# A Mamba block beside a mixture of experts: two products, then two scans on VectorE, and B's spreads as jobs in the ring of three banks

## The chip, the cores and the metric

The kernel runs on one core of one Trainium2 chip. The metric is device time of one execution, in microseconds (us). Three executions of the kernel before took 312.34, 308.81 and 311.08 us: median 311.08.

## The reference, cut to what matters

The input is 8 sequences of 256 tokens with 128 features, so 2048 tokens. All is float32.

```
xn = layernorm(x)
# s: Mamba block on xn
xr = rmsnorm(xn) * norm_w;   xi, z = split(xr @ W_in)          # 256 channels each
xc = silu(causal_conv4(xi) + conv_b)
dt, B, C = split(xc @ W_x, [64, 80]);   dt = softplus(dt @ W_dt + b_dt)
h[t] = exp(dt * A) * h[t-1] + (dt * xc * B)[t]                  # 256 channels x 16 states
y = (sum over states of h * C + D_skip * xc) * silu(z);   s = xn + y @ W_out
# g: eight experts, the best two of each token, on xn
p = softmax(xn @ Wg);  scores = top-2 of p, normalised to sum 1
g = silu(sum over e of scores[e] * (relu(xn @ W1[e] + b1[e]) @ W2[e] + b2[e]))
out = x + s * g
```

## The kernel before, in words

The tokens go in 4 chunks of 512 tokens (two sequences). Channels times states of a chunk are 4096 recurrences. They are laid on 128 partitions as 4 states by 32 channels, two blocks of 32 channels to an instruction, so one **unit** is 128 partitions by 1024 elements and a chunk has 16 units, 64 in all. A pair of blocks (pair 0 to 3) meets four quads of states. Two units in a row, on two pairs, share a quad and so a spread of B.

A unit n passes through five steps on four engines:

- ScalarE makes the decays: two `decay` instructions of 128x512, `exp(negA * dt)` (L561), into `dec`, a ring of three.
- TensorE spreads four rows of B over the partitions: `spread_B` (L998), one matmul of 512 columns for two units, into one of the two PSUM banks `pB`.
- VectorE multiplies `dt*xc` by that B (`times_B`, the **product**, L879) into the two banks `pdbu`, and runs the **scan** (L892) over `dec` and `pdbu` into `hs`, a ring of three.
- GpSimd multiplies by C (`times_C`, L390) into `hc`, a ring of four.
- TensorE sums over the states in the bank `py` (`reduce`, L1017), for two units at once.

`dt` and `dt*xc` reach the partitions as `rep`, repeated by DMAs of 32 partitions (`replicas`, L321), eight for each pair.

Every engine has its own queue and works it in order; semaphores are the only links. The order is written out in slots. A chunk has 32 slots; before the change VectorE runs the product of unit n in slot 2n and its scan in slot 2n+1. Everything else is a **job** or a **step** that TABLE or STEPS puts in a slot: `tr` and `tn` transposes, `xc0`, `xc1` convolution, `z0`, `z1`, `dt`, `v0`, `v1` projections, `gl`, `gs`, `gb` gate and expert bias, `m0a` to `m7b` first and `y0` to `y7` second layers of experts, `o` output. TensorE fills each job (`fill`) into one of three PSUM banks `px`, by turns in the order of the list JOBS, and ScalarE (or VectorE: `by_dve`) empties it (`empty`). A job can be filled only when the job three places ahead of it in JOBS has been emptied:

```
dst = px[j % AUX]
if j >= AUX:
    wait_emptied(pe, *JOBS[j - AUX])
```

The product waits for the scan ahead of it, since both use the same `pdbu`, and the scan waits for its product:

```
dve.wait_ge(scan_done, n)          # in times_B(n)
dve.wait_ge(dbu_done, n + 1)       # in scan(n)
if n >= HS_RING:
    dve.wait_ge(hc_done, n - HS_RING + 1)
```

The router's part on VectorE is `gate`, a generator of five steps for a chunk, whose small instructions wait for one another one by one (`link`). `silu` (slot 10 or 11 of a chunk) has ScalarE load a table, run the SiLUs of the next chunk's `xc` and `z`, and load the table of exp and log again. Ahead of the slots stands a start-up part, PRE_JOBS, which makes the first unit of decays and products from `d0`, `d1`, `x0`, `x1` without `rep`; `keep_busy` has TensorE run matmuls whose result is not used.

## Time and profile before

| | |
|---|---|
| median of three executions | 311.08 us (308.81 to 312.34) |
| the profiled execution | 309.04 us |
| its span, first to last instruction | 307.2 us |
| busy: TensorE, VectorE | 276.6 us, 275.8 us |
| busy: GpSimd, ScalarE | 236.9 us, 224.3 us |
| 64 scans, 63 products on VectorE | 146.2 us, 77.3 us |
| 63 products by C on GpSimd | 149.2 us |
| first scan starts, last scan ends | 30.48 us, 296.83 us |

The busy time of an engine counts each moment once, so instructions that overlap do not count twice. TensorE's matmuls are pipelined and their ends are modelled: its real load is read from the starts of rows that follow one another. In the rows below, square brackets at the end of a row are the idle time of its engine ahead of it and what ended it.

### The profile page before, as it was taken

What the parts mean: (1) busy time and instruction counts of PE and PEld (TensorE: products, weight loads), DVE (VectorE), ACT (ScalarE), POOL (GpSimd) and SP (SyncE); (2) the same over time, 40 slices, a digit from 0 to 9 for tenths busy, and PEclk for the clock granted to TensorE, in tenths of its full rate; (3) what the DMA queues carried; (4) which work ended last, traced back from release to release, by engine and by line L of the source; (5) the groups of instructions that cost most, each with busy time, mean ns of one, the idle gap of its engine ahead of it and who ended that gap; (6) DMA issues with size and microseconds to landing.
All of it is one profiled execution on the core that took longest, in us unless ns stands there. A gap on an engine that the chain in (4) does not pass through costs nothing. (4 is left out here: it accounts for less than half of the span.)

```text
span 307.2 us, 4290 instructions
## 1 busy us (share of the span) xinstructions
PE 276.6 (90%) x1273; PEld 144.9 (47%) x1273; DVE 275.8 (90%) x317; ACT 224.3 (73%) x440; POOL 236.9 (77%) x184
## 2 busy tenths in 40 slices
PE   7996689989999999698999999799998799997992
PEld 5633234534726453136645554235762555561662
DVE  4778899949999999999999899999999999999993
ACT  1495496799994948999688686999666684696640
POOL 6327966359899975667999887668999688869893
PEclk9999979999999999999999999799999999999999
DMA  6938980006065830041470660050938600000002
GB/s 185 292 97 182 231 191 10 0 6 137 0 154 132 194 73 0 0 122 21 104 172 1 139 138 1 4 137 11 206 67 185 150 0 2 0 0 1 3 0 68
DMA packets 16630, 26.23 MB, mean 85 GB/s; under 512 B 4264, under 2 KB 9759, under 8 KB 16608
## 3 DMA queue, kind: packets, MB, share of 16 engines
q1 hardware_dynamic: 15794, 24.78, 34.5%
q0 software_dynamic: 384, 1.05, 1.5%
q8 instruction: 10, 0.16, 0.2%
q10 hardware_dynamic: 430, 0.14, 0.2%
q14 instruction: 12, 0.10, 0.1%
HBM read 8.00 MB, written 1.18 MB: 30 GB/s over the span
## 5 line engine op out<-in xcount | busy, mean ns | idle before, releaser
L390 POOL TENSOR_TENSOR hc<-hs,Ct 128x1024 f32<-128x1024 f32 x63 | 149.2, 2377 | 24.3 <-DVE hs L892 23.9
L892 DVE TENSOR_TENSOR_SCAN hs<-dec,pdbu 128x1024 f32<-128x1024 f32 x64 | 146.2, 2285 | 9.2 <-ACT dec L561 5.1
L561 ACT ACTIVATE dec<-rep,negA 128x512 f32<-128x512 f32 x126 | 86.9, 725 | 7.0 <-DMA rep<-dt_u 4.7
L879 DVE TENSOR_TENSOR pdbu<-rep,pB 128x1024 f32<-128x1024 f32 x63 | 77.3, 1228 | 5.5
L1119 PE MATMUL px<-xnT,w 128*128 128x512 f32 x128 | 64.6, 606 | 6.8 <-ACT xnT L624 2.8
L1125 PEld LDWEIGHTS px<-w,hT 128*128 128x128 f32 x512 | 60.8, 192 | 18.5 <-issue 9.4
L1125 PE MATMUL px<-w,hT 128*128 128x128 f32 x512 | 62.7, 277 | 3.0 <-ACT hT L690 3.0
L690 ACT ACTIVATE hT<-px,cols 128x512 f32<-128x512 f32 x64 | 43.5, 689 | 21.3 <-PE px L1125 10.7
L506 POOL TENSOR_TENSOR acc<-acc,ysc 128x512 f32<-128x512 f32 x29 | 37.6, 1297 | 17.6 <-ACT ysc L679 17.3
L679 ACT ACTIVATE ysc<-px,score 128x128 f32<-128x128 f32 x116 | 32.9, 371 | 14.6 <-PE px L1125 14.5
L1017 PE MATMUL py<-hc,rsel 128*32 128x512 f32 x256 | 39.2, 609 | 2.3 <-POOL hc L390 2.2
L1119 PEld LDWEIGHTS px<-xnT,w 128*128 128x128 f32 x128 | 21.9, 192 | 34.5 <-issue 16.5
L998 PE MATMUL pB<-dtp,sel 128*128 128x512 f32 x64 | 34.3, 618 | 0.5 <-DVE pdbu L879 0.5
L1069 PE MATMUL px<-xrT,wtap 128*128 128x512 f32 x56 | 25.4, 595 | 0.0
L998 PEld LDWEIGHTS pB<-dtp,sel 128*128 128x128 f32 x64 | 10.6, 189 | 19.3 <-issue 16.2
L1017 PEld LDWEIGHTS py<-hc,rsel 128*32 128x32 f32 x256 | 6.1, 109 | 27.4 <-issue 16.1
L1069 PEld LDWEIGHTS px<-xrT,wtap 128*128 128x128 f32 x56 | 10.2, 188 | 11.9 <-issue 10.6
L1076 PE MATMUL px<-xc,wx 128*96 128x512 f32 x16 | 9.3, 714 | 5.6 <-ACT xc L577 4.2
L647 ACT ACTIVATE xv<-px,cols 128x512 f32<-128x512 f32 x6 | 4.1, 686 | 10.6 <-PE px L1069 10.6
L397 POOL TENSOR_TENSOR zr<-zr,xv 128x512 f32<-128x512 f32 x6 | 7.6, 1275 | 4.6 <-DVE xv L853 4.6
L514 POOL TENSOR_TENSOR hs<-hs,hc 128x512 f32<-128x512 f32 x2 | 2.5, 1280 | 10.4 <-ACT hc L717 10.4
L1006 PE MATMUL py<-xc,skip 128*128 128x512 f32 x16 | 9.1, 655 | 1.4 <-DVE sz L901 1.4
(155 smaller groups left out, 275.5 us busy)
## 6 DMA issues: line engine op xcount, KB each, us to landing
rep<-dt_u SPq DMA_DIRECT2D x120, 128.0 KB, 2.4
Ct<-c_rows SPq DMA_DIRECT2D x16, 256.0 KB, 5.0
w<-in_L_ffn_W SPq DMA_DIRECT2D x1, 1024.0 KB
rep<-dt_u POOLq DMA_DIRECT2D x8, 128.0 KB, 4.6
...
```

The lines of the kernel that those rows point to most:

```text
L390: eng.tensor_tensor(hc[:, n % HC_RING], hs[:, n % HS_RING], Ct[:, k % 2, j:j + 1, :].to_broadcast([P, 2, CH]), ALU.mult).then_inc(hc_last ...
L506: pool.tensor_tensor(acc[:, k % 2, :], acc[:, k % 2, :], ysc[:, pool_experts.index((k, e)) % YSC_RING, :], ALU.add).then_inc(acc_added, 1)
L561: act.activation(dec[:, n % DEC_RING, i, :], rep[:, q, 0, :], ACT.Exp, scale=negA[:, q, j:j + 1])\
L679: ins = act.activation(ysc[:, m % YSC_RING, t], src[:, t], ACT.Copy, scale=score[:, k % 2, i, e:e + 1])
L690: ins = act.activation(hT[:, e % 2, b, :], src[:, :], ACT.Relu, bias=cols[:, V_B1 + HB * e + b:V_B1 + HB * e + b + 1])
L879: dve.tensor_tensor(pdbu[:, :, :], rep[:, 2 * pair:2 * pair + 2, 1, :], pB[:, m % 2:m % 2 + 1, :].to_broadcast([P, 2, CH]), ALU.mult).then ...
L892: dve.tensor_tensor_scan(hs[:, n % HS_RING].rearrange("p b t -> p (b t)"), dec[:, n % DEC_RING].rearrange("p b t -> p (b t)"), pdbu[:, :, ...
L998: pe.matmul(pB[:, m % 2, :], sel[:, j].rearrange("p s d -> p (s d)"), dtp[:, k % 2, :], start=True, stop=True)\
L1017: last = pe.matmul(py[r:r + GD, 0, :], rsel[:, :], hc[:, n % HC_RING, i, :], start=False, stop=j == QUADS - 1)
L1069: last = pe.matmul(dst[:, :], wtap[:, t, b * P:(b + 1) * P], xrT[:, :, t:t + SEQ], start=t == 0, stop=t == TAPS - 1)
L1119: last = pe.matmul(dst[:, :], w1[:, e, b * P:(b + 1) * P], xnT[:, k % 2, :], start=True, stop=True)
L1125: last = pe.matmul(dst[:, i * D:(i + 1) * D], hT[:, e % 2, b, i * P:(i + 1) * P], w2[:, e, b, :], start=b == 0, stop=b == HB - 1)
```

## The change

- **VectorE's order.** `at_slot` puts the products of units 2m and 2m+1 in slots 4m and 4m+1 and their scans in slots 4m+2 and 4m+3. `pdbu` has four banks, two for even and two for odd units; a product waits for the scan two units back.
- **B.** `spread_B` and the banks `pB` are gone. The spread for units 2m and 2m+1 is a job `B` in the ring `px`, ahead of the other jobs of slot 4m-2. Nothing empties it but the second product that reads it: its bank comes free when product 2m+1 is done.
- **Start.** `rep` of pair 0 of the first chunk is made by four matmuls (`u0`, `u1`, `e0`, `e1`) and four copies on ScalarE instead of eight DMAs, of which SP issued four and GpSimd four. The first scan stands ahead of the second half's `correction` on VectorE. Eleven of the sixteen matmuls of `keep_busy` go.
- **Tables.** Jobs and steps get new slots. `gate` is 15 steps of one instruction each. The memset of the far value is a step of its own (`far`). `reduce` of units 2i and 2i+1 moves from slot 4i+6 to 4i+7. The last load of the SiLU table moves from slot 124 to 129.

```
-PRE_JOBS = ["tr", "xc0", "xc1", "dt", "x0", "v0", "x1", "v1", "d0", "d1", "tn", "m0a"]
+PRE_JOBS = ["tr", "xc0", "xc1", "dt", "x0", "v0", "B", "x1", "v1", "d0", "d1", "tn", "u0", "u1", "e0", "e1", "m0a"]
...
-    3: ["tr"], 6: ["z1"], 7: ["xc0", "z0"], 9: ["xc1"], 12: ["y0", "y1", "dt"], 13: ["m3a", "tn", "v0"],
...
+    3: ["tr"], 7: ["xc1"], 9: ["xc0", "z0", "z1"], 12: ["dt"], 13: ["y0", "tn", "v0"], 15: ["y1", "gl"], 16: ["m2a"],
...
 START = {
-    "second": [0], "gate": [2, 3, 4, 4, 7], "gate_e": [0], "gate_p": [1, 3, 5],
+    "second": [1], "gate": [1, 1, 3, 3, 5, 5, 5, 5, 6, 7, 7, 8, 8, 8, 10], "gate_e": [0], "gate_p": [1, 7, 7],
 }
+AHEAD = 2
 LEAD = 2
-LAG = 5
+LAG = 7
...
-BUSY = {"row": 8, "rows": 4, "tr": 2, "xc1": 2}
+BUSY = {"row": 3, "xc1": 2}
...
+for m in range(1, UNITS // HALF_PAIRS):
+    SLOTS.setdefault(4 * m - AHEAD, []).insert(0, ("B", m))
...
+def at_slot(n):
+
+    m, r = divmod(n, 2 * HALF_PAIRS)
+    scans = (1, 3) if m == 0 else (2, 3)
+    return r in scans, HALF_PAIRS * m + (r // 2 if m == 0 else r % 2)
...
-        pB = banks("pB", 2)
-        pdbu = banks("pdbu", 2)
+        pdbu = banks("pdbu", 4)
...
         def wait_emptied(eng, job, k):
 
-            if by_dve(job, k):
+            if job == "B" and k > 0:
+                eng.wait_ge(dbu_done, HALF_PAIRS * (k + 1))
+            elif by_dve(job, k):
...
-                dve.wait_ge(B_spread, m + 1)
-                if j == first_quad(k, pair):
+                if j == 0:
                     wait_replicas(dve, k, pair)
-                dve.wait_ge(scan_done, n)
-                dve.tensor_tensor(pdbu[:, :, :], rep[:, 2 * pair:2 * pair + 2, 1, :], pB[:, m % 2:m % 2 + 1, :].to_broadcast([P, 2, CH]),
-                                  ALU.mult).then_inc(dbu_done, 1)
+                if n > 1:
+                    dve.wait_ge(scan_done, n - 1)
+                if m == 0:
+                    wait_emptied(dve, "B", 0)
+                    B = B_first
+                else:
+                    wait_filled(dve, "B", m)
+                    B = bank_of("B", m)
+                at = 2 * (n % 2)
+                dve.tensor_tensor(pdbu[:, at:at + 2, :], rep[:, 2 * pair:2 * pair + 2, 1, :],
+                                  B[:, None, :].to_broadcast([P, 2, CH]), ALU.mult).then_inc(dbu_done, 1)
...
                 if n < 2 * UNITS:
-                    scan(n // 2) if n % 2 else times_B(n // 2)
+                    scanned, unit = at_slot(n)
+                    scan(unit) if scanned else times_B(unit)
...
+                elif job in ("u0", "u1"):
+                    pe.wait_ge(u_done, 1)
+                    last = pe.matmul(dst[:, :], copies(int(job[1])), dt_u[:, 0, 1, :], start=True, stop=True)
+                elif job in ("e0", "e1"):
+                    pe.wait_ge(far_done, 1)
+                    last = pe.matmul(dst[:, :], copies(int(job[1])), dt_u[:, 0, 0, :], start=True, stop=True)
...
-                if n % 4 == 3 and n // 4 + 2 < UNITS // HALF_PAIRS:
-                    spread_B(n // 4 + 2)
-                if n % 4 == 2 and 0 <= (n - LAG) // 4 < UNITS // 2:
+                if (n - LAG) % 4 == 0 and 0 <= (n - LAG) // 4 < UNITS // 2:
                     reduce((n - LAG) // 4)
```

**VectorE, from the end of the first chunk into the second,** around the steps `gate_y` (L901, L931 now) and `o` (L917, L947 now). L879 and L908 now are products, L892 and L922 now are scans; `px1` is a bank of the ring. Before:

```order
L901 TENSOR_TENSOR sz<-py,sz 128x512
L892 SCALAR_TENSOR_TENSOR hs<-dec,pdbu 128x1024
L879 TENSOR_TENSOR pdbu<-rep,pB 128x1024
L892 SCALAR_TENSOR_TENSOR hs<-dec,pdbu 128x1024
L917 TENSOR_TENSOR xn<-px1,xn 128x512
L879 TENSOR_TENSOR pdbu<-rep,pB 128x1024
L892 SCALAR_TENSOR_TENSOR hs<-dec,pdbu 128x1024
L879 TENSOR_TENSOR pdbu<-rep,pB 128x1024
L892 SCALAR_TENSOR_TENSOR hs<-dec,pdbu 128x1024
```

Now:

```order
L931 TENSOR_TENSOR sz<-py,sz 128x512
L884 MEMSET dt_u 128x2
L922 SCALAR_TENSOR_TENSOR hs<-dec,pdbu 128x1024
L947 TENSOR_TENSOR xn<-px2,xn 128x512
L908 TENSOR_TENSOR pdbu<-rep,px1 128x1024 x2
L922 SCALAR_TENSOR_TENSOR hs<-dec,pdbu 128x1024 x2
L908 TENSOR_TENSOR pdbu<-rep,px2 128x1024 x2
L922 SCALAR_TENSOR_TENSOR hs<-dec,pdbu 128x1024 x2
```

Products and scans now come two and two, and each two products read one bank of the ring.

**TensorE, slots 5 to 13 of the first chunk,** where the next chunk's convolution is done. L998 before and L1118 now spread B; L1069 and L1093 are a convolution, L1076 and L1100 the job `dt`, L1017 and L1041 `reduce`, L1125 and L1161 a `y`. Before:

```order
L998 MATMUL pB<-dtp,sel 128x512
L1069 MATMUL px2<-xrT,wtap 128x512 x4
L1055 MATMUL px0<-xrT,win 128x512
L1107 MATMUL px1<-ident,score 32x128
L1069 MATMUL px2<-xrT,wtap 128x512 x4
L1017 MATMUL py<-hc,rsel 32x512 x4
L998 MATMUL pB<-dtp,sel 128x512
L1113 MATMUL px0<-b2d,sT 128x512
L1125 MATMUL px1<-w2,hT 128x128 x8
L1125 MATMUL px2<-w2,hT 128x128 x8
L1076 MATMUL px0<-xc,wx 96x512 x2
```

Now:

```order
L1118 MATMUL px1<-dtp,sel 128x512
L1030 MATMUL py<-xc,skip 128x512
L1041 MATMUL py<-hc,rsel 32x512 x4
L1093 MATMUL px2<-xrT,wtap 128x512 x4
L1093 MATMUL px0<-xrT,wtap 128x512 x4
L1079 MATMUL px1<-xrT,win 128x512
L1079 MATMUL px2<-xrT,win 128x512
L1118 MATMUL px0<-dtp,sel 128x512
L1143 MATMUL px1<-ident,score 32x128
L1041 MATMUL py<-hc,rsel 32x512 x4
L1149 MATMUL px2<-b2d,sT 128x512
L1100 MATMUL px0<-xc,wx 96x512 x2
```

The two convolutions and `z0`, `z1` now all stand between two spreads of B, and `dt` stands in the bank of the next B, so it waits for that B's products.

**ScalarE, right behind the SiLUs of the second chunk.** L561 before and L570 now are decays, L679 and L692 the scaling of an expert's output. Before:

```order
L581 ACT_TABLE_LOAD
L683 ACTIVATE acc<-px0 128x512
L561 ACTIVATE dec<-rep,negA 128x512
L679 ACTIVATE ysc<-px1,score 128x128 x4
L679 ACTIVATE ysc<-px2,score 128x128 x4
L652 ACTIVATE dtp<-px0 96x512
L561 ACTIVATE dec<-rep,negA 128x512
```

Now:

```order
L590 ACT_TABLE_LOAD
L696 ACTIVATE acc<-px2 128x512
L570 ACTIVATE dec<-rep,negA 128x512
L661 ACTIVATE dtp<-px0 96x512
L570 ACTIVATE dec<-rep,negA 128x512
L692 ACTIVATE ysc<-px1,score 128x128 x4
```

The two experts' scalings no longer stand between the two decays of unit 8.

## Rows read from the trace of the kernel before

**Rows 1.** The cores: span, and mean granted TensorE clock.

```profile
core 0: 307.2 us, clock 0.988
```

**Rows 2.** The page: busy us (share of the span) and instructions of each engine.

```profile
PE 276.6 (90%) x1273; PEld 144.9 (47%) x1273; DVE 275.8 (90%) x317; ACT 224.3 (73%) x440; POOL 236.9 (77%) x184
```

**Rows 3.** Windows: us, busy of PE, PEld, DVE, ACT, POOL (instructions), clock, DMA share, GB/s.

```profile
36.63:296.83 260.20, 241.62 (x1138) 124.88 (x1139) 242.77 (x231) 206.16 (x409) 210.85 (x129) 0.99 0.31 71
296.83:307.20 10.37, 4.84 (x39) 3.50 (x37) 5.37 (x12) 0.63 (x1) 4.89 (x3) 0.97 0.18 51
```

**Rows 4.** VectorE by line: busy, mean ns of one, idle ahead of them and its releaser.

```profile
L892 DVE TENSOR_TENSOR_SCAN hs<-dec,pdbu 128x1024 f32<-128x1024 f32 x64 | 146.2, 2285 | 9.2 <-ACT dec L561 5.1
L879 DVE TENSOR_TENSOR pdbu<-rep,pB 128x1024 f32<-128x1024 f32 x63 | 77.3, 1228 | 5.5
```

**Rows 5.** VectorE in order of time: start us, us, line, operation, tiles.

```profile
139.18 2.27 DVE L892 TENSOR_TENSOR_SCAN hs<-dec,pdbu 128x1024 f32<-128x1024 f32 x1
141.37 0.16 DVE L824 TENSOR_REDUCE gmx<-px 128x4 f32<-128x32 f32 x1
...
147.32 0.18 DVE L829 TENSOR_REDUCE gsm<-gex 128x4 f32<-128x32 f32 x1
147.54 0.18 DVE L830 RECIPROCAL gri<-gsm 128x4 f32<-128x4 f32 x1
...
155.78 1.23 DVE L879 TENSOR_TENSOR pdbu<-rep,pB 128x1024 f32<-128x1024 f32 x1
156.92 0.56 DVE L845 TENSOR_TENSOR goh<-iota,gif 128x64 f32<-128x64 f32 x1
...
161.22 2.29 DVE L892 TENSOR_TENSOR_SCAN hs<-dec,pdbu 128x1024 f32<-128x1024 f32 x1
163.61 1.23 DVE L879 TENSOR_TENSOR pdbu<-rep,pB 128x1024 f32<-128x1024 f32 x1
164.93 2.29 DVE L892 TENSOR_TENSOR_SCAN hs<-dec,pdbu 128x1024 f32<-128x1024 f32 x1
```

**Rows 6.** In order of time, all engines, 63 to 68 us.

```profile
63.85 2.17 ACT L679 ACTIVATE ysc<-px,score 128x128 f32<-128x128 f32 x8
...
66.33 0.75 ACT L561 ACTIVATE dec<-rep,negA 128x512 f32<-128x512 f32 x1
...
67.11 2.29 DVE L892 TENSOR_TENSOR_SCAN hs<-dec,pdbu 128x1024 f32<-128x1024 f32 x1 [4.51 <-ACT dec L561]
```

**Rows 7.** TensorE in order of time, 169 to 179 us.

```profile
169.41 1.95 PE L1125 MATMUL px<-w,hT 128*128 128x128 f32 x16
171.19 0.60 PE L1049 MATMUL px<-ident,rl 128*128 128x128 f32 x4
...
172.77 1.07 PE L1017 MATMUL py<-hc,rsel 128*32 128x512 f32 x8
173.77 3.70 PE L1069 MATMUL px<-xrT,wtap 128*128 128x512 f32 x8
177.31 1.02 PE L998 MATMUL pB<-dtp,sel 128*128 128x512 f32 x2
178.16 1.02 PE L1055 MATMUL px<-xrT,win 128*128 128x512 f32 x2
```

**Rows 8.** Window of 20 us, columns as in rows 3.

```profile
160.00:180.00 20.00, 20.00 (x104) 11.75 (x103) 18.36 (x13) 14.61 (x35) 18.60 (x13) 1.00 0.43 96
```

**Rows 9.** GpSimd by line.

```profile
L390 POOL TENSOR_TENSOR hc<-hs,Ct 128x1024 f32<-128x1024 f32 x63 | 149.2, 2377 | 24.3 <-DVE hs L892 23.9
```

**Rows 10.** Windows of 2 us around a pause of TensorE.

```profile
192.00:194.00 2.00, 0.20 (x2) 0.22 (x2) 1.81 (x3) 1.99 (x3) 1.88 (x1) 1.00 0.00 0
194.00:196.00 2.00, 2.00 (x3) 0.59 (x3) 1.90 (x2) 1.98 (x3) 0.65 (x2) 0.50 0.00 0
```

**Rows 11.** ScalarE in order of time: the first decays from rep.

```profile
32.67 1.33 ACT L561 ACTIVATE dec<-rep,negA 128x512 f32<-128x512 f32 x2 [2.23 <-DMA rep<-dt_u]
...
36.43 0.72 ACT L561 ACTIVATE dec<-rep,negA 128x512 f32<-128x512 f32 x1 [2.42 <-DMA rep<-dt_u]
```

More of the change, by code:

```diff
@@ L93 @@
+OWN = {"o"} | {f"{a}{i}" for a in "xdue" for i in range(2)} | {f"y{e}" for e in range(EXPERTS)} | {f"m{e}{b}" for e in range(EXPERTS) for b in "ab"}
 SLOTS = {n: [(j, 0) for j in EARLY[n]] for n in EARLY}
@@ L238, in mamba_moe @@
         c_out, c_in = sem("c_out"), [sem(f"c_in{i}") for i in range(2)]
-        rep_in, rep_soft = [sem(f"rep_in{i}") for i in range(PAIRS)], [sem(f"rep_soft{i}") for i in range(HALF_PAIRS)]
+        rep_in, rep_soft = [sem(f"rep_in{i}") for i in range(PAIRS)], sem("rep_soft")
         e_done, l_done = sem("e_done"), sem("l_done")
@@ L258, in mamba_moe @@
         ov_dram = out.rearrange("b (h p) d -> p (b h) d", p=P)
-        order_a = [job for job in JOBS if not by_dve(*job)]
+        order_a = [job for job in JOBS if not by_dve(*job) and (job[0] != "B" or job[1] == 0)]
         order_v = [job for job in JOBS if by_dve(*job)]
@@ L300, in wait_added @@
                 eng.wait_ge(acc_added, pool_experts.index((k, e)) + 1)
-        def first_quad(k, pair):
-            return 1 if (k, pair) == (0, 0) else 0
         def wait_replicas(eng, k, pair):
-            early = pair < HALF_PAIRS
-            eng.wait_ge(rep_in[pair], N_REP * (k + 1) - (N_REP // 2 if early else 0))
-            if k == 0 and early:
-                eng.wait_ge(rep_soft[pair], N_REP // 2)
+            if (k, pair) == (0, 0):
+                wait_emptied(eng, "e1", 0)
+            elif (k, pair) == (0, 1):
+                eng.wait_ge(rep_in[1], N_REP // 2)
+                eng.wait_ge(rep_soft, N_REP // 2)
+            else:
+                eng.wait_ge(rep_in[pair], N_REP * (k + (pair > 1)) + (N_REP // 2 if pair == 1 else 0))
         def decays(n):
@@ L374, in _ @@
                 for pair in range(PAIRS):
-                    repeat_dt_u(k, pair ^ 1 if k == 0 and pair < HALF_PAIRS else pair)
+                    if (k, pair) != (0, 0):
+                        repeat_dt_u(k, pair)
             for k in range(CHUNKS):
@@ L515, in _ @@
             pool.wait_ge(far_done, 1)
-            for q in (3, 1):
-                replicas(pool, q, True)
+            replicas(pool, 3, True)
             rest_roots()
@@ L555, in decay @@
                 k, j, pair = place(n)
-                if j == first_quad(k, pair) and i == 0:
+                if j == (1 if n < HALF_PAIRS * QUADS and pair == 0 else 0) and i == 0:
                     wait_replicas(act, k, pair)
@@ L612, in empty @@
             def empty(job, k):
-                if job[-1] == "<" or by_dve(job, k):
+                if job[-1] == "<" or job == "B" or by_dve(job, k):
                     return
@@ L740, in _ @@
                     empty(job, k)
+                for _ in steps_at(n, "last_table"):
+                    assert n >= 2 * (UNITS - LEAD) - 1
+                    act.preload_act_table_set("silu_and_others")
+                    silu_of_experts(CHUNKS - 2)
                 for k, b in steps_at(n, "log1p"):
@@ L828, in gate @@
                 dve.wait_ge(gate_exp, k + 1)
-                link(dve.tensor_reduce(gsm[:, :], gex[:, :, :], AX.X, ALU.add))
-                link(dve.reciprocal(gri[:, :], gsm[:, :]))
+                dve.tensor_reduce(gsm[:, :], gex[:, :, :], AX.X, ALU.add).then_inc(gate_step, 1)
+                yield
+                dve.wait_ge(gate_step, done + 2)
+                dve.reciprocal(gri[:, :], gsm[:, :]).then_inc(gate_step, 1)
                 yield
@@ L960, in _ @@
                     correction(k, b)
+                for k, b in steps_at(n, "far"):
+                    set_far(k, b)
                 for k, b in steps_at(n, "times_dt"):
@@ L986, in _ @@
             last.then_inc(cw_spread, 1)
[L987 removed]
             pe.wait_ge(w_rows, 16 * N_ROWS)
[L989 to L999 removed]
+            pe.transpose(pdbu[:, 2, 0:V_END], rows[:, :], ident[0:V_END, 0:V_END]).then_inc(vec_t, 1)
             def skip_xc(k, b):
@@ L1089, in fill @@
                                          start=True, stop=True)
+                elif job == "B":
+                    if k == 0:
+                        pe.wait_ge(selected, N_SELECTED)
+                    wait_emptied(pe, "dt", k // (DB * QUADS))
+                    last = pe.matmul(dst[:, :], sel[:, k % QUADS].rearrange("p s d -> p (s d)"),
+                                     dtp[:, k // (DB * QUADS) % 2, :], start=True, stop=True)
                 elif job in ("x0", "x1"):
```

112 lines of the change are left out of this document (53 added, 59 removed), and 26 rows, old and new, of the table TABLE.

## The prediction

> **What bounds the kernel now.** I read first the span and the totals, then the windows, then VectorE's lines, then its instructions in order of time. The span is 307.2 us [rows 1] and the profiled execution 309.04 us, so 1.84 us lie around it. TensorE and VectorE are both busy 90% [rows 2], which does not say which one sets the time. The windows say more: from the end of the second scan (36.63 us) to the end of the last (296.83 us) VectorE is busy 242.8 of 260.2 us, and behind it come 10.4 us of tail [rows 3]. VectorE's 17.4 idle us are what to look at. Its two big lines hold 9.2 + 5.5 us of them; only 5.1 us are put down to another engine, ScalarE's decays [rows 4]. The other 9.6 us have no releaser: VectorE waits for itself.
>
> The order of time shows how. A scan starts at 161.22 and takes 2.29 us; the product behind it, which needs its banks, starts at 163.61, 0.10 us after the scan's end; the next scan, which needs that product, starts at 164.93, 0.09 us after the product's end [rows 5]. A unit so takes 2.39 + 1.32 = 3.71 us. Where the instruction behind needs nothing of the one ahead, it starts before that one ends: the router's reduction at 141.37, 2.19 us after its scan's start; the comparison at 156.92, 1.14 us after its product's start [rows 5]. So a link from scan to product costs 0.20 us more than no link, one from product to scan 0.18 us more, and a unit without both takes 3.33 us. VectorE sets the time, and about a tenth of a unit is the wait for its own result.
>
> **The change, part by part.**
>
> *Two products, then two scans.* Every product and scan is then followed by an instruction that does not need it. Number of links that go: 5.5 us of idle ahead of products by 0.10 to 0.13 us is some 48; 4.1 us ahead of scans (9.2 less the 5.1) by 0.09 is some 45 [rows 4, 5]. At 0.20 and 0.18 us: 9.6 + 8.1 = 17.7 us. All lies on the path, since VectorE is it. The lower bound is that only the 9.6 us of idle go; nothing is excluded above 17.7. I take 17.7, by the two independent pairs.
>
> Here a rule speaks against the change. The Trainium skill (VectorE: DVE Perf Modes, The DRAIN you can't avoid) says that the next operation does not issue until the pipe is empty and that leaving out semaphores between operations won nothing. By that rule the links would be worth nothing. The page itself adds (Two Vector instructions with no wait between them) that an instruction that is not held starts earlier, and this case's trace agrees with that: 0.08 and 0.09 us before the end of the one ahead, against 0.09 and 0.10 us after it. The measurement decides.
>
> *The router in 15 steps, the far memset apart.* In a chunk some five small instructions wait for one another, like the reciprocal 0.04 us after the end of its reduction (147.50 to 147.54) [rows 5]. With a scan or product between them that is 0.12 us less each: 4 chunks by about 4 links, 2 us. Between 0 and 3; 2 taken.
>
> *The stall at 62 us.* VectorE's longest wait is 4.51 us for the second decay of unit 8, at 66.33 us: ScalarE had come out of its SiLUs and then did eight scalings, 2.17 us, and `dt` ahead of that decay [rows 6]. In the new order the scalings stand behind it, and the scan of unit 8 comes one slot later. This wait should go. What is late next is B: between the spreads for units 4, 5 and for units 8, 9, TensorE has two convolutions of 3.54 us, two `reduce` of 1.0 us, `y0` of 1.78 us, and nine matmuls of 512 columns and 0.85 us (`z0`, `z1`, `gb`, two for `dt`, `v0`, one of skip, two of B), with 0.6 us for transposes: 7.1 + 2.0 + 1.8 + 7.7 + 0.6 = 19.2 us [rows 7]. VectorE needs for four units 13.3 us, with the router 14.0. B runs ahead by 3 to 4 us at most, since its ring stands still until the products ahead are done. So B is late by 1.6 us or more; with the wait of `dt` for the SiLUs and for the bank of a B I take 2.5. Net 4.5 - 2.5 = 2 us won; bounds 0 and 4.5.
>
> *B in the ring.* Before, a spread had two banks of its own. Now it holds one of three from its fill until the second product is done, and TensorE can fill two more jobs behind it and then stands. Everything from the third job to the next B then has to fit under two scans and their company, 4.4 us and more. In most groups it does: three matmuls of 0.85 and a `y` of 1.78 with `reduce`. Where it doesn't, I count as above: behind spread 16 stand from the third job on `m7b`, `y6`, `tr`, `y7` and the next B, 0.85 + 1.78 + 0.6 + 1.78 + 0.85 = 5.9 us, under 5.0 us of scans and one output: 0.9 late; around 18 stand two convolutions again, 1.3 late. Over all 31 spreads, those of the stall above left out, this gives some 3.5 us. TensorE has little in reserve: 20.00 of 20 us busy at 160 to 180 us [rows 8]. Lower bound 0; upper bound by the `y` of 1.78 us that is the common piece, half of one late at every second spread, 14 us.
>
> *GpSimd and ScalarE.* The multiplication by C takes 2.38 us [rows 9], and a scan of an odd unit may start only when that of the unit two back is done. In steady state that one starts with the two products and has 1.14 + 1.14 + 2.19 = 4.5 us for 2.38, a slack of 2.1 us; before it was 3.71 + 1.32 - 2.38, about 2.7. Where an expert's addition and a sum for dt stand together it is used up. I take 1.2 us for such places, bounds 0 and 6. `reduce` a slot later costs nothing: it is hidden under the scans, and at the end its last part waits for the last C product, as before.
>
> *The start.* ScalarE waited 2.42 us for the replicas of pair 0 behind 2.23 us for those of pair 1 [rows 11]. The second wait goes, and eight DMAs with it, four issued by SP and four by GpSimd; for it ScalarE has four copies, of about a decay's 0.72 us, while it would wait for pair 1 anyway. SP's sixteen issues for pairs 2 and 3, queued behind, begin sooner or at the same time. The first wait stays, and with it the second product. As VectorE did the router's part in that time, I take 1 us, between 0 and 2.4. The eleven matmuls less of `keep_busy` I cost at nothing while the clock stays up; what it costs if it does not is a rival below. The tail of 10.4 us [rows 3] stays: the last four instructions of units 62, 63 end in the same chain.
>
> Sum, on the profiled execution: 309.0 - 17.7 - 2 - 2 + 3.5 + 1.2 - 1 = **291.0 us**. The median of before stands 2.0 us above the profiled execution and its runs 3.5 us apart, so for the median of after I say 292.
>
> **The rivals.**
>
> *B late at every spread: slower.* One B for each two units, 31 of them. The links, the router, the stall and the start are worth 20 to 23 us, so at 0.7 us late at each the gain is gone. One thing makes that possible: TensorE standing for a full ring. After 1.8 of 2 us without work (192 to 194 us) its granted clock was 0.50, that is 1.2 of its 2.4 GHz, in the next 2 us [rows 10], and a B and a convolution then take twice as long, while the ring is what made it stand. At 1.0 us each the time is 309 - 22.7 + 31 = 317 us. For it: TensorE's full window [rows 8], a ring now shared by 45 jobs a chunk instead of 37. Against it: counted by group, TensorE's work is less than VectorE's in most, and it can catch up in those. 8 in 100.
>
> *The links were worth nothing* (each instruction waits for the pipe anyhow): 309 - 2 - 1 + 4.7 = 311 us. For it speaks no row; the drain page of the Trainium skill would give this. 4 in 100.
>
> *GpSimd becomes the bound in places.* It is busy 210.9 of the 260.2 us [rows 3], 53 us a chunk; VectorE's chunk falls from 65 to about 60 us, and the load of GpSimd rises from 81% to 88%. Then 1 us waits at most groups that hold an expert's addition, some 8 of them more: 299 us; up to 304. For it: that load, in an order that is fixed. Against: it waited 23.9 us for scans. 14 in 100.
>
> *The clock falls at the start*, for want of the matmuls left out: the start-up's convolution and three or four matmuls on the path at half speed, 3.5 + 0.85 at least: 295 us. 6 in 100. The forecast keeps 68 in 100.
>
> **How the numbers follow.** The forecast's own range, by its bounds, is 284 (no late B, the whole stall gone) to 298. To hold 8 in 10 of all cases I go to 304, which takes in GpSimd's, and leave out the two at 311 and 317 and a little on the low side. About 1% (3 us) is what a measurement can tell. Faster by over that (below 308 us): 0.68 + 0.14 + 0.05, a little less for the unforeseen, 0.86; within: 0.06; slower: 0.08.
>
> **What would show it.** Two scans in a row 2.19 us apart, two products 1.14 us, and idle ahead of both lines without a releaser near 0: the first term right. Waits of product lines for TensorE's spread: the ring, 6 us in all if I am right, at 50 to 70 us and near the convolutions; over 20 us, the first rival. Waits of scans for GpSimd: the third. If products and scans stay 0.09 us behind the one ahead, the second. A clock below 0.9 in the first 25 us, the fourth. Most wrong I would be if many short waits, each for another engine, came in place of the links.

## The result, and the profile after

The changed kernel takes 295.99 us (median of four executions, 295.79 to 296.08), the kernel before 311.71 us beside it (308.81 to 312.74). The ratio is 0.951 (95% interval 0.944 to 0.958), so 5% faster. The profiled execution took 296.01 us against 309.04 us: 13.0 us less, where the forecast had 18.0 less. The time lies in the stated range (284 to 304 us), 4 us above the stated 292. By the medians the gain is 15.7 us, by the profiled executions 13.0: the one of the kernel before lies at the low end of its spread.

The rhythm came out as read. VectorE in order of time, changed kernel (columns as in [rows 5]):

```profile
243.27 2.32 DVE L908 TENSOR_TENSOR pdbu<-rep,px 128x1024 f32<-128x1024 f32 x2
245.51 4.45 DVE L922 TENSOR_TENSOR_SCAN hs<-dec,pdbu 128x1024 f32<-128x1024 f32 x2
249.88 2.32 DVE L908 TENSOR_TENSOR pdbu<-rep,px 128x1024 f32<-128x1024 f32 x2
252.12 4.45 DVE L922 TENSOR_TENSOR_SCAN hs<-dec,pdbu 128x1024 f32<-128x1024 f32 x2
256.54 2.36 DVE L908 TENSOR_TENSOR pdbu<-rep,px 128x1024 f32<-128x1024 f32 x2
```

Two units take 6.61 us (243.27 to 249.88) and 6.66 us, 3.32 us each; forecast 3.33, before 3.71 [rows 5]. Now its two big lines (as [rows 4]) and the windows (as [rows 3]), the middle one again from the end of the second scan to the end of the last:

```profile
L922 DVE TENSOR_TENSOR_SCAN hs<-dec,pdbu 128x1024 f32<-128x1024 f32 x64 | 144.1, 2272 | 0.6 <-ACT dec L570 0.4
L908 DVE TENSOR_TENSOR pdbu<-rep,px 128x1024 f32<-128x1024 f32 x62 | 73.5, 1217 | 13.6 <-PE px L1118 12.4 <-PE px L1143 1.1
```

```profile
36.65:283.71 247.06, 236.16 (x1140) 124.38 (x1139) 231.34 (x230) 205.78 (x404) 208.08 (x128) 0.99 0.32 73
283.71:294.20 10.49, 4.83 (x39) 3.48 (x37) 5.46 (x13) 0.63 (x1) 6.29 (x5) 0.96 0.17 50
```

The scans' idle time is 0.6 us against 9.2 [rows 4]. That of the products is 13.6 us against 5.5, and it is of another kind: 12.4 + 1.1 us have a releaser, TensorE. The stretch is 247.06 us against 260.20 [rows 3]. Neighbouring instructions now overlap by up to 0.1 us, and the windows' busy time does not add up with the gaps, so the idle time is taken from the gaps in order of time: 15.7 us, against 17.2 before. The waits for itself went, and waits for B came. The second scan ends at 36.65 us, as before (36.63), and the tail is 10.5 us, as before. GpSimd has not become a bound: no scan waits for it; it still waits for scans:

```profile
L400 POOL TENSOR_TENSOR hc<-hs,Ct 128x1024 f32<-128x1024 f32 x63 | 149.2, 2384 | 17.3 <-DVE hs L922 12.8 <-PE py L1041 4.5
```

Where the waits for B lie, in order of time on VectorE, those over 1 us:

```profile
52.37 2.36 DVE L908 TENSOR_TENSOR pdbu<-rep,px 128x1024 f32<-128x1024 f32 x2 [1.11 <-PE px L1143]
...
64.74 1.23 DVE L908 TENSOR_TENSOR pdbu<-rep,px 128x1024 f32<-128x1024 f32 x1 [5.64 <-PE px L1118]
...
185.80 2.36 DVE L908 TENSOR_TENSOR pdbu<-rep,px 128x1024 f32<-128x1024 f32 x2 [2.66 <-PE px L1118]
...
194.71 2.36 DVE L908 TENSOR_TENSOR pdbu<-rep,px 128x1024 f32<-128x1024 f32 x2 [2.18 <-PE px L1118]
```

They are at 52 to 65 us and 183 to 195 us, where the convolutions and the SiLUs of the next chunk are done. Five short ones (0.19 to 0.57 us) make the rest. The longest is one chain over TensorE and ScalarE:

```profile
56.87 2.71 PE L1100 MATMUL px<-xc,wx 128*96 128x512 f32 x4 [2.45 <-ACT xc L586]
...
57.70 1.28 ACT L590 ACT_TABLE_LOAD   x1
...
59.38 2.87 PE L1161 MATMUL px<-w,hT 128*128 128x128 f32 x16
...
60.10 0.58 ACT L661 ACTIVATE dtp<-px 96x512 f32<-96x512 f32 x1
...
62.52 1.02 PE L1106 MATMUL px<-dtp,wdt 128*128 128x512 f32 x2
...
63.48 1.12 PE L1118 MATMUL px<-dtp,sel 128*128 128x512 f32 x2
```

`dt` starts 2.45 us late for the SiLUs and, at a granted clock of 0.50, the lower level of 1.2 GHz, takes 2.71 us; `y0` (16 matmuls from 59.38) takes 2.87; `v0` and then B follow. VectorE stands from 59.10 to 64.74 us. The windows of 2 us (columns as in [rows 3]) show the clock behind TensorE's pause:

```profile
54.00:56.00 2.00, 0.42 (x1) 0.00 (x0) 2.00 (x2) 1.99 (x3) 0.42 (x1) 1.00 0.00 0
56.00:58.00 2.00, 1.13 (x3) 0.58 (x4) 2.00 (x2) 1.98 (x3) 1.00 (x1) 0.97 0.00 0
58.00:60.00 2.00, 2.00 (x5) 0.96 (x4) 1.10 (x1) 1.99 (x3) 1.35 (x1) 0.50 0.00 0
60.00:62.00 2.00, 2.00 (x15) 2.00 (x14) 0.00 (x0) 1.29 (x3) 0.00 (x0) 0.68 0.07 16
```

### The profile page after: what moved, and what is told of

It reads as the page before. It is cut to its first block and busy times, and to the rows that moved or that the text cites. A ratio compares the mean times of both kernels' runs of the same rounds, so it can differ in the third digit from the quotient of the medians.

```text
span 294.2 us, 4278 instructions
## 1 busy us (share of the span) xinstructions
PE 274.6 (93%) x1259; PEld 144.0 (49%) x1259; DVE 264.6 (90%) x317; ACT 228.8 (78%) x444; POOL 235.0 (80%) x180
## 5 line engine op out<-in xcount | busy, mean ns | idle before, releaser
L400 POOL TENSOR_TENSOR hc<-hs,Ct 128x1024 f32<-128x1024 f32 x63 | 149.2, 2384 | 17.3 <-DVE hs L922 12.8
L922 DVE TENSOR_TENSOR_SCAN hs<-dec,pdbu 128x1024 f32<-128x1024 f32 x64 | 144.1, 2272 | 0.6 <-ACT dec L570 0.4
L570 ACT ACTIVATE dec<-rep,negA 128x512 f32<-128x512 f32 x126 | 85.5, 722 | 0.8 <-DMA rep<-dt_u 0.8
L908 DVE TENSOR_TENSOR pdbu<-rep,px 128x1024 f32<-128x1024 f32 x62 | 73.5, 1217 | 13.6 <-PE px L1118 12.4
L1161 PEld LDWEIGHTS px<-w,hT 128*128 128x128 f32 x512 | 62.1, 194 | 16.7 <-issue 8.7
L1161 PE MATMUL px<-w,hT 128*128 128x128 f32 x512 | 63.9, 279 | 0.5 <-DVE pdbu L908 0.5
L692 ACT ACTIVATE ysc<-px,score 128x128 f32<-128x128 f32 x116 | 33.1, 368 | 13.9 <-PE px L1161 13.7
L1041 PE MATMUL py<-hc,rsel 128*32 128x512 f32 x256 | 35.6, 605 | 0.0
L1118 PE MATMUL px<-dtp,sel 128*128 128x512 f32 x64 | 33.3, 601 | 0.5 <-ACT xnT L633 0.5
L1093 PE MATMUL px<-xrT,wtap 128*128 128x512 f32 x56 | 26.7, 624 | 0.0
L1093 PEld LDWEIGHTS px<-xrT,wtap 128*128 128x128 f32 x56 | 10.9, 201 | 14.5 <-issue 14.4
L1118 PEld LDWEIGHTS px<-dtp,sel 128*128 128x128 f32 x64 | 11.1, 190 | 12.9 <-issue 8.2
L1041 PEld LDWEIGHTS py<-hc,rsel 128*32 128x32 f32 x256 | 5.4, 108 | 22.4 <-issue 15.1
L1100 PE MATMUL px<-xc,wx 128*96 128x512 f32 x16 | 8.4, 653 | 6.8 <-ACT xc L586 6.8
L1106 PE MATMUL px<-dtp,wdt 128*128 128x512 f32 x16 | 8.5, 615 | 0.9 <-issue 0.5
```

Source lines behind the costliest of these rows:

```text
L400: eng.tensor_tensor(hc[:, n % HC_RING], hs[:, n % HS_RING], Ct[:, k % 2, j:j + 1, :].to_broadcast([P, 2, CH]), ALU.mult).then_inc(hc_last ...
L570: act.activation(dec[:, n % DEC_RING, i, :], rep[:, q, 0, :], ACT.Exp, scale=negA[:, q, j:j + 1])\
L692: ins = act.activation(ysc[:, m % YSC_RING, t], src[:, t], ACT.Copy, scale=score[:, k % 2, i, e:e + 1])
L908: dve.tensor_tensor(pdbu[:, at:at + 2, :], rep[:, 2 * pair:2 * pair + 2, 1, :], B[:, None, :].to_broadcast([P, 2, CH]), ALU.mult).then_inc ...
L922: dve.tensor_tensor_scan(hs[:, n % HS_RING].rearrange("p b t -> p (b t)"), dec[:, n % DEC_RING].rearrange("p b t -> p (b t)"), pdbu[:, at: ...
L1041: last = pe.matmul(py[r:r + GD, 0, :], rsel[:, :], hc[:, n % HC_RING, i, :], start=False, stop=j == QUADS - 1)
```

## The experiments

Times are medians unless said otherwise; each kernel is the changed one with the edit shown, compared with it (296.0 us) or with one another. A **link** is the wait of a product or a scan for the instruction just ahead of it on VectorE. **The stretch** is the time from the end of the second scan to the end of the last in the profiled execution: 260.20 us in the kernel before, 247.06 in the changed one. It leaves out the start, which differs between executions: in runs 4, 7, 8 and 9, which have the changed kernel's start, the second scan ends at 35.5 to 36.0 us, in the changed kernel's profiled execution at 36.65.

**1. Product and scan by turns, four banks kept.**

```
-    m, r = divmod(n, 2 * HALF_PAIRS)
-    scans = (1, 3) if m == 0 else (2, 3)
-    return r in scans, HALF_PAIRS * m + (r // 2 if m == 0 else r % 2)
+    return n % 2 == 1, n // 2
```

> The changed kernel (296.0 us) with product and scan by turns again (product of unit n in slot 2n, scan in slot 2n+1), the four banks kept: the link from product to scan is back, that from scan to the next product is not, since that product uses the other pair. Theory (the links are the gain): some 45 links by 0.18 us, 8 us, and a bank of the ring is held one scan (2.2 us) longer for each B, so B is late more often, 3 to 8 us: 307 to 312 us; products start 0.09 us before the scan ahead ends, scans 0.09 us after their product. Rival (the links are worth nothing, the gain lies in the new tables and the start): 295 to 298 us.

Measured: 342.4 us in the fastest of four executions, which is the profiled one, 46 us over the changed kernel; the others took 348.2 to 354.3 us (median 351.2). Both theories missed by far. VectorE by line:

```profile
L920 DVE TENSOR_TENSOR_SCAN hs<-dec,pdbu 128x1024 f32<-128x1024 f32 x64 | 146.2, 2285 | 6.5 <-ACT dec L568 2.5 <-issue 0.4
L906 DVE TENSOR_TENSOR pdbu<-rep,px 128x1024 f32<-128x1024 f32 x62 | 75.4, 1217 | 42.9 <-PE px L1116 38.7 <-PE px L1141 4.0
```

The products' idle time is 42.9 us, 29 us more than in the changed kernel, in 21 waits for TensorE instead of nine. Of the other 17 us, 5.9 are idle time ahead of the scans (2.5 of it for a decay), 4.0 busy time of these two lines, and 5.7 waits for other jobs of the ring. The product of the odd unit, which frees the bank of B, comes one scan (2.3 us) later, and the next B, filled behind the jobs that waited for that bank, is wanted after one scan instead of two. So the order of VectorE is not only worth its links: product, product, scan, scan leaves the time in which B can live in the ring. That is read from the order; no run tries the other order with a longer ring. The first rival of the prediction is a real mechanism; the changed kernel escapes it by its order.

**2. The same with one pair of banks.** As 1, and

```
-                if n > 1:
-                    dve.wait_ge(scan_done, n - 1)
+                dve.wait_ge(scan_done, n)
...
-                at = 2 * (n % 2)
+                at = 0
```

> As the alternate order, and with one pair of banks for all units, so that each product waits for the scan just ahead: both links back, all other parts of the change kept. Theory: 8 to 10 us more than the alternate order with four banks (45 to 50 links by 0.20 us), less what is absorbed by waits for B: 313 to 320 us, slower than the kernel before, because the ring is paid for without its return. Rival (links worth nothing): equal to the alternate order within 1 us.

Measured: 348.1 us in the fastest of four executions, 358.3 to 358.7 in the others; 313 to 320 us were expected. The fastest executions of 1 and 2 are 5.7 us apart, less than the 8 to 10 expected; with spreads this wide that is no measure of the link. Runs 5 and 6 took its place.

**3. Without the 31 spreads.** The products from the third unit on multiply by their own old banks, so the values are not the reference's. ScalarE's copy of `dt` no longer waits for a spread either.

```
-for m in range(1, UNITS // HALF_PAIRS):
-    SLOTS.setdefault(4 * m - AHEAD, []).insert(0, ("B", m))
...
-                else:
-                    wait_filled(dve, "B", m)
-                    B = bank_of("B", m)
...
+                                  B[:, None, :].to_broadcast([P, 2, CH]) if m == 0 else pdbu[:, at:at + 2, :],
```

> The changed kernel without the 31 spreads of B in the ring; a product takes its own old banks in PSUM in place of B, so the values are not the reference's from the third unit on, and the product keeps its operands' places (one in SBUF, one in PSUM) and its size. Theory (what is missing to the forecast is the wait of products for B, 13.5 us in the profile of the changed kernel, against 6 forecast): that wait goes and nothing takes its place, 282 to 285 us. Rival (ScalarE and GpSimd, busy 78% and 80%, take over as soon as B does not wait): 288 to 293 us, with waits of scans for decays or C products.

Measured: 290.8 us (290.2 to 291.4): 5.2 us less, not 11 to 14; the stretch is 242.37 us, 4.7 less. The rival was right. The two long waits on VectorE:

```profile
63.95 1.34 DVE L869 SCALAR_TENSOR_TENSOR xv<-xv,ev 128x512 f32<-128x512 f32 x1 [6.08 <-ACT xv L595]
...
191.42 2.29 DVE L917 TENSOR_TENSOR_SCAN hs<-dec,pdbu 128x1024 f32<-128x1024 f32 x1 [4.83 <-ACT dec L568]
```

At the first place, where products waited 5.64 us for B, a correction now waits 6.08 us for ScalarE, which gets there through `dt`, `y0` and `v0`. At the second, a scan waits 4.83 us for a decay, where B had taken 2.7 + 2.2. So the spreads cost 5 us net. The other 8 us of the waits for B stand on top of a chain of the next chunk that is as late without B. The run also takes the spreads' own work off TensorE (31 by 0.85 us by [rows 7]), which the kernel before had too; what the ring alone costs is not shown.

**4. Three spreads earlier.**

```
-    SLOTS.setdefault(4 * m - AHEAD, []).insert(0, ("B", m))
+    SLOTS.setdefault({4: 13, 19: 73, 20: 76}.get(m, 4 * m - AHEAD), []).insert(0, ("B", m))
...
-    "silu": [11], "log1p": [13, 17], "correct": [16, 20], ...
+    "silu": [11], "log1p": [13, 17], "correct": [17, 20], ...
```

> The changed kernel with three spreads moved ahead of the job they were queued behind: B of units 8, 9 ahead of y0, tn and v0 (slot 13), B of units 38, 39 ahead of the second convolution (slot 73), B of units 40, 41 ahead of m1a and v0 (slot 76); one correction step moves from slot 16 to 17. Theory (a spread needs nothing of those jobs; it is late for its place in TensorE's queue alone): the waits of 5.6, 2.7 and 2.2 us fall to under 1.5 us each, 287 to 290 us. Rival (the ring's turn is what counts: what is moved behind the spread is now late itself, and the decays or the next spread with it): 293 to 297 us.

Measured: 299.5 us (298.2 to 299.7), 3.5 us slower (the stretch 251.55 us, 4.5 more); both theories fell. In order of time on VectorE:

```profile
60.31 2.36 DVE L908 TENSOR_TENSOR pdbu<-rep,px 128x1024 f32<-128x1024 f32 x2 [2.35 <-PE px L1118]
67.67 0.19 DVE L832 TENSOR_REDUCE gmx<-px 128x4 f32<-128x32 f32 x1 [4.99 <-PE px L1112]
...
195.31 2.36 DVE L908 TENSOR_TENSOR pdbu<-rep,px 128x1024 f32<-128x1024 f32 x2 [5.73 <-PE px L1118]
```

The wait for the first B fell from 5.64 to 2.35 us, and the router then waits 4.99 us for its logits: their job now stands behind a `v0` that has the bank of B. Around 190 us there is one wait of 5.73 us for B instead of 2.66 and 2.18. An earlier B blocks the ring for longer.

**5 and 6. The links by themselves: run 3 in the two other orders.** The same edits as 1 and 2, on the kernel without spreads, in which nothing waits for a bank that B holds.

> The kernel without the 31 spreads (290.8 us; a product takes its own old banks in place of B), with product and scan by turns and the four banks kept. Nothing waits for a bank of the ring here, so only the link from product to scan comes back. Theory (0.18 us each, some 45 of them, and 3 us fewer waits for ScalarE since VectorE is slower): 296 to 299 us. Rival (the links are worth nothing or the order matters for another reason): 290 to 292 us, or over 305 us.

> As the run without spreads in alternate order, with one pair of banks, so that each product also waits for the scan just ahead: both links. Theory: 8 to 10 us over that run (45 to 50 links by 0.20 us), 305 to 308 us, 15 to 18 us over the run without spreads that has neither link. Rival (the link from scan to product is hidden by the waits for ScalarE): within 2 us of the alternate order with four banks.

Measured: 302.8 us (302.5 to 302.9) and 307.2 us (305.9 to 307.8), against 290.8 us with neither link. Both links together are worth 16.4 us, in the range given (15 to 18); they did not split as expected: 12.0 for the one from product to scan, so that run 5 lies between its theory (296 to 299 us) and its rival (over 305), and 4.4 for the other, where 8 to 10 were expected. The stretches are 242.37, 253.03 and 257.31 us: 10.7 and 4.3, 14.9 in all. By line, run 3, 5 and 6:

```profile
L917 DVE TENSOR_TENSOR_SCAN hs<-dec,pdbu 128x1024 f32<-128x1024 f32 x64 | 143.9, 2271 | 6.1 <-ACT dec L568 5.9
L902 DVE TENSOR_TENSOR pdbu<-rep,pdbu 128x1024 f32<-128x1024 f32 x62 | 73.2, 1212 | 0.0
```

```profile
L915 DVE TENSOR_TENSOR_SCAN hs<-dec,pdbu 128x1024 f32<-128x1024 f32 x64 | 146.2, 2284 | 9.6 <-ACT dec L566 6.1
L900 DVE TENSOR_TENSOR pdbu<-rep,pdbu 128x1024 f32<-128x1024 f32 x62 | 75.0, 1209 | 0.0
```

```profile
L914 DVE TENSOR_TENSOR_SCAN hs<-dec,pdbu 128x1024 f32<-128x1024 f32 x64 | 146.2, 2285 | 9.8 <-ACT dec L566 6.2
L899 DVE TENSOR_TENSOR pdbu<-rep,pdbu 128x1024 f32<-128x1024 f32 x62 | 76.0, 1226 | 2.4
```

The waits for other engines on these lines and the correction's are 12.0, 12.8 and 11.0 us in the three (scans 5.9, 6.1 and 6.2; correction 6.1, 6.7 and 4.8), so they do not explain 16.4 us. The links do. Idle time without a releaser is 3.5 us ahead of the scans in run 5, and 3.6 + 2.4 us in run 6. The rest is not idle time: an independent instruction starts before the end of the one ahead, and with the link this overlap is lost. Where nothing else stands between products and scans, a unit takes 3.31 us in run 3 (two from 244.15 to 250.76), 3.50 us in run 5 (248.23 to 251.73) and 3.64 us in run 6 (248.16 to 251.80), against 3.71 in the kernel before [rows 5]. In run 6 the product there starts 0.03 us behind its scan, where it was 0.10 in the kernel before, so this run prices that link low.

From run 3 to 5 the two lines give 3.5 + 2.3 + 1.8 = 7.6 us of the stretch's 10.7. Of what is left, 2.0 us are two other lines that ran longer (the correction 962 ns instead of 793, 7 times; `times_dt` 913 instead of 800, 8 times), and 0.8 us are longer waits for other engines. These lengths differ between runs of one order too (927 and 862 ns in run 6), so they are not put down to the link. The second scan ends at 36.59 us in run 5, at 35.53 in run 3 and at 35.61 in run 6, which has run 5's order: 1.1 us of what the medians give to the link from product to scan can be the start. From run 5 to 6 the gaps from scan to product turn from 3.6 us of overlap into 2.2 us of idle time and the products take 1.0 us longer; the correction waits 1.8 us less and some lines run shorter, which leaves 4.3.

**7. `y0` behind `v0`.**

```
-    12: ["dt"], 13: ["y0", "tn", "v0"], 15: ["y1", "gl"], ...
+    12: ["dt"], 13: ["tn", "v0"], 15: ["y0", "y1", "gl"], ...
```

> The changed kernel with y0 of the first chunk moved from slot 13, where it stands ahead of tn and v0, to slot 15, behind them and behind the spread of units 8 and 9. Theory (VectorE's stall of 5.6 us at 59 to 65 us is the chain SiLU, table, dt, its copy, y0 on TensorE at half clock, v0, and then B; y0 is the piece that need not be in it, 2.7 us): 2 to 3 us less, 293 to 294 us. Rival (what comes next, the second layer of the expert or the first correction, takes the gain): 295.5 to 296.5 us.

Measured: 295.5 us (294.7 to 295.7), 0.5 us less (the stretch 246.44 us, 0.6 less). The wait for B fell from 5.64 to 3.88 us, and 2.0 us of waiting for the router's logits came. The rival was right.

**8. The same, TensorE kept busy while `dt` waits.**

```
+                    for _ in range(WARM if k > 0 else 0):     # WARM = 9
+                        pe.matmul(dst[:, 0:P], ident[:, :], ident[:, :], start=True, stop=True)
```

> As the run with y0 moved, and TensorE runs nine matmuls of 128x128 on the bank of dt (their result is overwritten) while it waits for the SiLUs, in chunks 2 to 4. Theory (the granted clock was 0.50 at 58 to 60 us after a pause of 2.5 us, and dt took 2.71 us there against 1.93 at full clock): another 0.8 to 2 us less, 291.5 to 293 us; clock 1.00 at 56 to 62 us. Rival (the pause is too short in the other chunks and the matmuls only delay dt): 0 to 1 us more than the run with y0 moved.

Measured: 294.4 us (294.1 to 294.6), 1.1 us under run 7 and clear of its range; both theories missed. Three of the windows above:

```profile
54.00:56.00 2.00, 2.00 (x19) 2.00 (x19) 2.00 (x2) 2.00 (x3) 0.02 (x1) 1.00 0.00 0
58.00:60.00 2.00, 0.44 (x3) 0.27 (x2) 0.08 (x1) 2.00 (x4) 2.00 (x2) 1.00 0.00 0
60.00:62.00 2.00, 2.00 (x8) 0.56 (x11) 0.15 (x1) 1.86 (x4) 0.64 (x1) 1.00 0.07 16
```

The granted clock stays at 1.00 (2.4 GHz), and `dt` takes 1.88 us, where it took 3.28 in run 7 and 2.71 in the changed kernel. The wait for B stays all the same (3.77 us against 3.88 in run 7): TensorE now stands 1.56 us for ScalarE's copy of `dt`, which comes behind the table load, `gb` and a decay. So the clock did not hold this chain; ScalarE did. Nor is the 1.1 us found there: the stretch is 246.33 us, 0.11 less than in run 7, and 0.37 of the 0.48 us between the two profiled executions lie ahead of it, where the edit changes nothing. What the higher clock is worth here is not shown.

**9. As 8, two spreads right behind `dt`.**

```
-    SLOTS.setdefault(4 * m - AHEAD, []).insert(0, ("B", m))
+    SLOTS.setdefault({4: 13, 20: 76}.get(m, 4 * m - AHEAD), []).insert(0, ("B", m))
```

> As the run with y0 moved and TensorE kept busy (294.4 us), and the spreads of units 8, 9 and of units 40, 41 moved ahead of v0, right behind dt (slots 13 and 76). With y0 gone from there v0 takes the bank of dt and does not wait for that spread. Theory (the spread needs neither v0 nor the copy of dt that ScalarE makes behind its table load): the products' waits of 3.8 and 2.2 us fall under 1 us each; half of it comes back as a wait for the router's logits or for ScalarE: 290 to 292.5 us. Rival (v0 and the first correction behind it are what is late; VectorE then waits there for as long): 294 to 295 us.

Measured: 298.8 us (298.5 to 300.6), 4.4 us slower than run 8. The waits for the spreads went as said (0.68 us at the first place, none at the second). The correction then waits 3.47 us, and 8 us later:

```profile
63.74 0.69 DVE L873 SCALAR_TENSOR_TENSOR xv<-xv,ev 128x512 f32<-128x512 f32 x1 [3.47 <-ACT xv L598]
...
71.92 0.19 DVE L833 TENSOR_REDUCE gmx<-px 128x4 f32<-128x32 f32 x1 [6.35 <-PE px L1115]
```

```profile
65.62 5.47 PE L1164 MATMUL px<-w,hT 128*128 128x128 f32 x32 [3.50 <-DVE pdbu L909]
```

TensorE stood 3.50 us for the second product to free the bank, with `y0`, `y1` and the router's job behind it, and its next matmuls, `y0` and `y1`, ran 5.47 us where they took 3.84 in run 8. The product was itself behind the correction. This and run 4 are the same lesson.

**10. The idle matmuls of the start put back.** These are the matmuls of `keep_busy`, whose result is not used; each shows as two records in the rows.

```
-BUSY = {"row": 3, "xc1": 2}
+BUSY = {"row": 8, "tr": 2, "xc1": 2}
...
+            keep_busy(4)
             pe.wait_ge(w_rows, 16 * N_ROWS)
```

> The changed kernel with the eleven idle matmuls of the start put back (eight, four, two and two instead of three, none, none and two). Theory (their loss cost nothing while the clock stays up): 295.7 to 296.3 us. Rival (the clock of the first 20 us suffers): 1 to 3 us less.

Measured: 300.0 us (297.2 to 300.8), 4 us more, of which 2.6 us lie ahead of the end of the second scan. Both theories fell: leaving them out was a gain. TensorE's first rows, in the kernel before, the changed one and this one:

```profile
2.02 3.79 PE L979 MATMUL pB<-ident 128*128 128x128 f32 x16 [2.02 <-POOL iota L415]
5.73 2.22 PE L985 MATMUL pdbu<-hc,ones_row 1*128 1x512 f32 x4
7.89 1.16 PE L979 MATMUL pB<-ident 128*128 128x128 f32 x8
...
9.14 0.44 PE L1043 MATMUL px<-ident,rl 128*128 128x128 f32 x2
```

```profile
2.02 1.65 PE L1014 MATMUL pdbu<-ident 128*128 128x128 f32 x6 [2.02 <-POOL iota L425]
3.73 3.77 PE L1020 MATMUL pdbu<-hc,ones_row 1*128 1x512 f32 x4
...
7.48 0.69 PE L1067 MATMUL px<-ident,rl 128*128 128x128 f32 x2
```

```profile
2.02 3.78 PE L1014 MATMUL pdbu<-ident 128*128 128x128 f32 x16 [2.02 <-POOL iota L425]
5.73 3.78 PE L1020 MATMUL pdbu<-hc,ones_row 1*128 1x512 f32 x4
9.44 2.08 PE L1014 MATMUL pdbu<-ident 128*128 128x128 f32 x8
...
11.67 0.69 PE L1068 MATMUL px<-ident,rl 128*128 128x128 f32 x2
```

Sixteen idle records hold TensorE until 5.8 us in two of them. In this execution of the kernel before the spread of the taps then took 2.22 us; in the other two 3.78 us, and the eight idle records behind it 2.08 instead of 1.16 us. The first transposes start at 9.14, 7.48 and 11.67 us, the first scan at 30.17 us in run 10 against 27.53 in the changed kernel. So idle matmuls cost their own time on the path, and did not buy the higher speed.

**11. The router's steps grouped again.** The 15 slots of `gate` become five groups in each chunk, as for the last one shown:

```
-    "gate": [21, 21, 24, 25, 26, 27, 27, 27, 27, 27, 27, 27, 27, 27, 30],
+    "gate": [21, 21, 25, 25, 27, 27, 27, 27, 27, 27, 27, 27, 27, 27, 30],
```

> The changed kernel with the router's 15 steps put together again as the five groups of before (maxima, reciprocals and indices in a row, each linked to the one ahead). Theory (0.12 us for each link that comes back, three a chunk): 1 to 2 us more, 297 to 298 us. Rival (the waits for B absorb it): 295.8 to 296.3 us.

Measured: 296.4 us (295.9 to 296.9), 0.4 us more: between the two, nearer the rival. The stretch of the profiled execution is 248.24 us, 1.2 more, as the theory had it; the run doesn't decide between them.

**12. Pair 0 by DMA again.**

```
-..., "tn", "u0", "u1", "e0", "e1", "m0a"]
+..., "tn", "m0a"]
...
-                    if (k, pair) != (0, 0):
-                        repeat_dt_u(k, pair)
+                    repeat_dt_u(k, pair ^ 1 if k == 0 and pair < HALF_PAIRS else pair)
...
-            replicas(pool, 3, True)
+            for q in (3, 1):
+                replicas(pool, q, True)
```

> The changed kernel with pair 0 of the first chunk repeated by eight DMAs again, as before, instead of four matmuls and four copies. Theory (the second decay waits some 2.4 us for the DMAs, VectorE has the router's part to do meanwhile): 1 us more, up to 2.4, 296.5 to 298.4 us. Rival (ScalarE's four copies cost as much as the wait): 295.5 to 296 us.

Measured: 300.5 us (two executions at 299.0 and 299.1, two at 301.8), 3 to 6 us more; over both theories. ScalarE, TensorE and VectorE, in an execution of 301.8 us:

```profile
37.13 0.72 ACT L567 ACTIVATE dec<-rep,negA 128x512 f32<-128x512 f32 x1 [2.36 <-DMA rep<-dt_u]
...
38.60 2.08 PE L1115 MATMUL px<-dtp,sel 128*128 128x512 f32 x2 [3.02 <-ACT hT L700]
...
40.81 2.36 DVE L905 TENSOR_TENSOR pdbu<-rep,px 128x1024 f32<-128x1024 f32 x2 [2.41 <-PE px L1115]
```

ScalarE waits 2.36 us for pair 0, and an expert's job behind that decay is emptied late, so the spread that follows three places behind it is, too: TensorE stands 3.02 us for it. Behind this pause the granted clock is 0.50 (38 to 42 us), and the spread takes 2.08 us, not the 1.02 us of [rows 7]. The product waits 2.41 us for B. In the ring a late decay reaches VectorE a second time, through B.

## Why the prediction was right, and by how much it was off

**Links (17.7 us).** Right. Rows: no such gap is left, and the rhythm is 3.32 us. By runs 3 and 6 they are worth 16.4 us by the medians, 14.9 by the stretch. The Trainium skill (VectorE: DVE Perf Modes, The DRAIN you can't avoid) has it that chaining without semaphores saves nothing; in these runs, with operations of 1.2 and 2.3 us, the orders with and without the waits differ by 16.4 us (runs 6 and 3), and one order with and without the wait from scan to product by 4.4 us (runs 6 and 5). The measurement decides.

**Router and memset (2 us).** Rather too much by the one run on it: putting the five groups back costs 0.4 us by the medians and 1.2 by the stretch (run 11); it does not put back their old slots. The memset was not tried by itself.

**The stall at 62 us (4.5 gone, 2.5 in its place).** This step failed. The wait moved from the decay to the product and grew from 4.51 to 5.64 us. I counted TensorE's work between two spreads and took ScalarE as relieved of the scalings. The chain runs through both: SiLU, table load, copy of `dt`, `v0`, B. Runs 3, 7, 8 and 9 each take out one piece, and in each VectorE still waits over 3 us there, for B (7 and 8) or for the correction's input (3 and 9).

**B in the ring (3.5 us).** Mis-sized: the waits for B outside the stall are 13.6 - 5.6 = 8.0 us, of which 1.1 us at 52 us and 4.8 us at 183 to 195 us, where I had 1.3 for two convolutions. Net of what else would be late the spreads cost 5.2 us, their own work on TensorE included (run 3).

**GpSimd and ScalarE (1.2 us).** Too much: no scan waits for GpSimd, and the scans' waits for ScalarE are 0.4 us.

**The start (1 us), idle matmuls (nothing).** The first was near, as far as can be told. The second scan ends at the same time, and the fourth earlier; it in the kernel before, then in the changed one:

```profile
44.07 2.29 DVE L892 TENSOR_TENSOR_SCAN hs<-dec,pdbu 128x1024 f32<-128x1024 f32 x1
```

```profile
41.63 2.28 DVE L922 TENSOR_TENSOR_SCAN hs<-dec,pdbu 128x1024 f32<-128x1024 f32 x1
```

It ends at 43.91 us against 46.36, 2.45 less; two units' links are 0.76 of it, so 1.7 us are left for the start. The end of the second scan differs by up to 1.1 us between profiled executions with the same start (35.52 us in run 4, 36.65 in the changed kernel), so this figure is no better than that, and up to 1 us of the 5 us missing to the forecast can be such a difference. But the start hangs on more than I priced: put back alone, the idle matmuls cost 4 us (run 10), and the replicas of pair 0 3 to 6 us (run 12), through the ring.

**The account.** From the end of the second scan to the end of the last it is 13.1 us less, and the gaps on VectorE explain it. Idle time: 9.3 us of links, the 4.5 us stall and 3.4 us of short waits went; 13.6 us for B, 0.4 us for a decay and 1.7 us of others came, 1.5 less. Time in which VectorE works: 11.6 less. Of that 8.4 are an estimate for the overlap, the forecast's count of 93 links by 0.09 us (instructions now start 0.08 to 0.11 us ahead of the end of the one before them; the 0.10 us behind it is in the idle time), 1.5 us are shorter scans and products (2272 ns for 2285, 1217 for 1228); 1.7 us are not told apart, the router's steps among them. So the links gave 17.7 us by this account and 16.4 or 14.9 by runs 3 and 6, and what the forecast had too low is B: 13.6 us of waits for it, where it had 6. That the total is off by 5 us and not by these 7.6 is in part luck: 3.4 us of short waits and 1.5 us of instruction lengths went that were in no term, and the 1.2 us for GpSimd and ScalarE came only in part.

**The rivals.** Links worth nothing: refuted by runs 3 to 6. GpSimd as the bound: no row shows it. B late at every spread: run 1 alone comes near it, with 21 waits at the 31 spreads, 42.9 us in all. The clock at the start: the matmuls there were slow in the profiled execution, but with the idle matmuls they are too (run 10), so the rival had its cause wrong.

No experiment beat the changed kernel by much. Runs 7 and 8 are under it in time (295.5 and 294.4 against 296.0 us), in other sessions, and their ratios to the kernel before, 0.955 (0.947 to 0.963) and 0.951 (0.944 to 0.959), do not tell them from its 0.951.
